# A transformer block on one core: last chunk of batch 1 finished inside the MLP, first search in other banks, second search's last turn one block later

## The chip, the cores and the metric

The kernel runs on one core of a Trainium2 chip. The metric is device time in microseconds (us); before the change it is 2070.14 us, the median of 3 runs (2069.56 to 2070.2). Engines are named as in the profile: PE multiplies matrices, DVE and ACT work on tiles, POOL does small vector work and issues indirect DMAs, SP issues plain DMAs.

## The reference

Two batches of 4096 tokens, 256 features, float32. A tokenizer with a 4096 x 4096 gate, then attention over heads with gates, then a feed-forward layer through which only the best half of the tokens goes:

```python
h = tok(x)                                    # (2, 4096, 256)
h = h + attn(layernorm(h))                    # 8 heads, sigmoid gate, residual
z = layernorm(h)
weights = z @ wr + br                         # one router weight for each token
_, idx = top_k(weights, 2048); sel_idx = idx[:, :2047]
y = (gelu(z[sel_idx] @ w1 + b1) @ w2 + b2) * w_sel      # hidden width 1024
out = h + z;  out[sel_idx] += y
```

## The kernel before

The tokenizer and the weights of the heads fill the first 1670 us or so and are not touched here. Two stages follow.

**mix** runs over 8 chunks of 512 tokens, both batches `s` = 0 and 1 in each (a tile row `[h, s]`, `h` being the parity of the chunk). PE makes values, gates and the output projection (`project`, into banks 0 to 3, `products`). For a chunk and batch DVE then runs `moments` (residual added to `rows`, mean and variance) and `route` (router weight, stored in `rows` and kept in `router`, counted by `mx_w_kept`); POOL runs `scale` between the two (reciprocal root of the variance, shift); ACT runs `norm` (the normalized row plus residual, `base`); SP stores `rows` to `scratch["rows"]` and `base` to the output. A chunk's batch 1 is finished two steps after it was begun, so (chunk 7, batch 1) comes last of all.

**mlp** takes the best tokens. `TopRows` finds them on DVE and PE for a batch `b`: ten turns; DVE counts (L1258, L1261), PE adds the counts over partitions (`pe_turn`, L1348), DVE goes on (`dve_advance`). Turns 0 to 7 find the threshold digit by digit, turn 8 the ranks, and turn 9 takes a large comparison on DVE (`dve_lanes`, L1317) and 32 small products on PE (L1354), from which `dve_list` makes the list of rows (`top_rows`). It uses `CB`, bank 2, and `TIES`, bank 3.

The first search (b = 0) runs alone (`dve_all(0)`), then POOL gathers the first three units of 512 rows (`gather(0)` to `gather(2)`, four indirect DMAs each), ACT normalizes unit 0 (`norm`), PE turns it (`turn`), ACT and DVE split it in high and low parts (`split`), and the MLP begins: 8 units `u` of 8 blocks `j`, in all 64 blocks, `g = 8u + j`. In this text H(g) is the first layer's product of block g (6 matmuls, L1588) and S(g) the second layer's (12 matmuls, L1568); PE's order is H(g), a turn of the second search if there is one, S(g - 2), and at j = 4 the turning of the next unit. Between H and S, ACT makes Gelu and its high part, DVE the low part `act_lo` (L1534). POOL's `base(u)` (L1428) adds the normalized rows to the gathered ones; `base(0)` stands behind `gather(2)` in POOL's order.

The second search (b = 1) is spread over these blocks: a stage on DVE at every second g (`search`), PE's turn n in block g = 2n + 2. Turn 9 is thus in block 20, its comparison on DVE in block 19, and the list in block 20. `gather(4)`, the first of batch 1, waits for that list.

Waits are on semaphores, in each engine's program order; the order is written by hand.

Of the kernel before, what the change touches and what calls it, by code (L numbers as in the profile page):

```python
# [5 lines left out]
P = 128  # L6
# [879 lines left out]
def mix(pr, W2, M, products, room, scratch, router, mlp_raw, W3):  # L886
# [3 lines left out]
    with ExitStack() as ctx:  # L890
        m_hi, m_lo, V, GB = (M[n] for n in ("m_hi", "m_lo", "V", "GB"))
        h_in, rows = (room[n] for n in ("h_in", "rows"))
        base, late = sb(nc, ctx, "base", [P, 2, 2, TPC, D]), sb(nc, ctx, "late", [P, 8 * CH])
# [15 lines left out]
        block = pr.block  # L909

# [50 lines left out]
        def _(act):  # L961
# [28 lines left out]
            def step(c, h):  # L990
# [3 lines left out]
                if within(c, 2):  # L994
                    norm(c - 2, h, 1)
# [15 lines left out]
            chunks(step)  # L1011

        @block.vector
        def _(dve):
# [45 lines left out]
            def step(c, h):  # L1060
                if within(c, 2):
                    moments(c - 2, h, 1)
# [4 lines left out]
                if within(c, 2):  # L1067
                    route(c - 2, h, 1)
# [12 lines left out]
            chunks(step)  # L1081

        @block.gpsimd
        def _(pool):
# [52 lines left out]
            def step(c, h):  # L1137
                if within(c, 2):
                    scale(c - 2, h, 1)
# [14 lines left out]
            chunks(step)  # L1154

        @block.tensor
        def _(pe):
# [29 lines left out]
            chunks(step)  # L1187

# [6 lines left out]
class TopRows:  # L1195
# [8 lines left out]
    def __init__(self, pr, W2, W3, router, sbuf, K):  # L1204
# [20 lines left out]
        self.CB, self.TIES = pr.banks[2], pr.banks[3]  # L1225
# [37 lines left out]
    def dve_advance(self, b, q):  # L1263
# [4 lines left out]
        link(v.scalar_tensor_tensor(self.reach[:, :], self.CB[:, 0:PIV], float(self.K), self.W3["step"][:, q % STEPS, :],  # L1268
# [90 lines left out]
def mlp(pr, W2, W3, ident, scratch, router):  # L1359
# [9 lines left out]
    with ExitStack() as ctx:  # L1369
# [16 lines left out]
        all_rows = scratch["rows"].rearrange("b c j p e -> (b c j p) e")  # L1386
        out_rows = pr.out.rearrange("b t d -> (b t) d")
# [22 lines left out]
        def _(pool):  # L1410
            def gather(u):
# [4 lines left out]
                for j in range(TPC):  # L1416
                    nc.gpsimd.indirect_dma_start(taken[:, u % HELD, j, :], None, all_rows, offsets(u, j)).then_inc(
# [13 lines left out]
            for u in range(HELD):  # L1431
# [12 lines left out]
        def _(act):  # L1444
# [14 lines left out]
            for b in range(B):  # L1459
                stored(act, b)  # L1460
            for j in range(TPC):
                norm(0, j)
            split(0)
            for u in range(U):
                for j in range(FT):
# [5 lines left out]
                    act.wait_ge(gelu_ok, u * FT + j + 1)  # L1471
# [7 lines left out]
        def _(dve):  # L1479
# [33 lines left out]
            def search(g):  # L1513
# [37 lines left out]
        def _(pe):  # L1551
# [164 lines left out]
```

## Time and profile before

| | |
|---|---|
| median of 3 runs | 2070.14 us |
| the profiled execution | 2072.95 us, its span 2071.2 us |
| busy, share of the span | PE 96%, DVE 59%, ACT 33%, POOL 22% |
| chain that ended last, by engine | PE 90%, DVE 4%, issue 2%, ACT 2%, POOL 1% |
| granted clock, mean over the span | 0.977 of full speed |

The span runs from the first to the last instruction; 1.75 us of the profiled execution lie around it. The granted clock is that of PE, as a share of 2.4 GHz: 0.50 is its lower level of 1.2 GHz. Times of rows are microseconds from the span's start.

### The profile page before, as it was taken

The numbers are of one execution on the slowest core, as the hardware profiler recorded it, in microseconds if no ns is written. First come the engines' busy times: TensorE is split into PE (matmuls) and PEld (weight loads), VectorE is DVE, ScalarE is ACT, GpSimd is POOL, SyncE is SP. The second block draws the span as 40 slices with busy tenths as digits, with TensorE's granted clock in tenths as the row PEclk, the third lists the DMA queues.
The fourth block names the chain that finished last, engine by engine and source line by source line (L and its number), as shares of the span: only waits on it lengthen the run. The fifth ranks groups of instructions, "written<-read, shape, count | busy, mean of one in ns | idle before, by whom it ended". The sixth has DMA issues, their size and how long they took to land.

```text
span 2071.2 us, 27479 instructions
## 1 busy us (share of the span) xinstructions
PE 1988.7 (96%) x9534; PEld 1646.7 (80%) x9534; DVE 1222.2 (59%) x2220; ACT 675.0 (33%) x1093; POOL 451.0 (22%) x578
## 2 busy tenths in 40 slices
PE   7999999999999999999999999999999989829998
PEld 6888888888888888888888888888887878718897
DVE  4656565665656556656565665656554358756553
ACT  4422222222222225422222222222222147524454
POOL 3302020202202023312020201202023057532342
PEclk9999999999999999999999999999999989959999
DMA  4232433334243333242433334243334469620110
GB/s 143 88 105 73 162 112 122 112 122 145 75 164 112 122 112 132 72 153 81 154 112 123 111 122 150 73 162 112 112 112 143 148 241 313 220 77 22 42 42 31
DMA packets 88114, 250.14 MB, mean 121 GB/s; under 512 B 11968, under 2 KB 32448, under 8 KB 88000
## 3 DMA queue, kind: packets, MB, share of 16 engines
q1 hardware_dynamic: 84928, 240.27, 34.5%
q0 software_dynamic: 3072, 8.44, 1.3%
q8 instruction: 61, 1.00, 0.2%
q14 instruction: 53, 0.43, 0.1%
HBM read 194.05 MB, written 54.62 MB: 120 GB/s over the span
## 4 chain that ended last, share of the span: by engine, by line
PE 90%; DVE 4%; issue 2%; ACT 2%; POOL 1%; DMA 0%; SPq 0%; DVEq 0%; ACTq 0%; POOLq 0%
PE bank L663 34%; PE bank L678 34%; PE bank L1568 4%; PE bank L810 4%; PE bank L1588 4%; PE bank L713 3%; PE bank L1169 2%; PE bank L635 1%; PE bank L609 1%; PE bank L619 1%; DVE kt L482 0%; DVE vf L493 0%; PE bank L648 0%; ACT work L380 0%; PE bank L836 0%
## 5 line engine op out<-in xcount | busy, mean ns | idle before, releaser
L678 PE MATMUL bank<-x_hi,kt 128*128 128x512 f32 x2048 | 724.0, 395 | 1.5 <-DVE work L519 1.4
L519 DVE SCALAR_TENSOR_TENSOR work<-bank,d_col,gate 128x512 f32<-128x512 f32 x512 | 383.8, 750 | 553.7 <-PE bank L678 544.7
L398 ACT ACTIVATE p_hi<-work 128x512 fp32r<-128x512 f32 x512 | 324.1, 633 | 1065.5 <-PE bank L663 1024.9
L678 PEld LDWEIGHTS bank<-x_hi,kt 128*128 128x128 f32 x2048 | 384.4, 188 | 90.4 <-DVE work L519 2.4
L663 PE MATMUL bank<-p_hi,v_hi 128*128 128x512 f32 x1024 | 407.0, 397 | 0.3 <-ACT yT L360 0.2
L663 PE MATMUL bank<-p_hi,v_lo 128*128 128x512 f32 x1024 | 404.2, 395 | 0.0
L663 PE MATMUL bank<-p_lo,v_hi 128*128 128x512 f32 x1024 | 403.4, 394 | 0.0
L678 PE MATMUL bank<-x_lo,kt 128*128 128x512 f32 x1024 | 401.0, 392 | 0.0
L507 DVE TENSOR_TENSOR p_lo<-work,p_hi 128x512 fp32r<-128x512 f32 x512 | 367.4, 718 | 29.3 <-ACT p_hi L398 29.2
L568 POOL TENSOR_SCALAR spread<-mv 128x4 f32<-128x4 f32 x16 | 4.9, 308 | 1125.4 <-DVE mv L451 1125.4
L663 PEld LDWEIGHTS bank<-p_hi,v_hi 128*128 128x128 f32 x1024 | 192.2, 188 | 50.6 <-DVE p_lo L507 5.3
L663 PEld LDWEIGHTS bank<-p_hi,v_lo 128*128 128x128 f32 x1024 | 192.3, 188 | 46.3
L663 PEld LDWEIGHTS bank<-p_lo,v_hi 128*128 128x128 f32 x1024 | 193.2, 189 | 44.7
L678 PEld LDWEIGHTS bank<-x_lo,kt 128*128 128x128 f32 x1024 | 192.3, 188 | 43.4
L1534 DVE TENSOR_TENSOR act_lo<-act,act_hi 128x512 fp32r<-128x512 f32 x64 | 59.2, 925 | 91.0 <-ACT act_hi L1472 90.8
L1568 PE MATMUL bank<-ffn,act_hi 128*128 128x256 f32 x512 | 97.4, 289 | 0.0
L1588 PE MATMUL bank<-fx_hi,ffn 128*128 128x512 f32 x256 | 92.5, 408 | 2.2 <-DVE fx_lo L1483 2.2
L1568 PEld LDWEIGHTS bank<-ffn,act_hi 128*128 128x128 f32 x512 | 84.2, 194 | 4.3 <-DVE act_lo L1534 0.2
L575 POOL TENSOR_TENSOR mn_sb<-mn_sb,gamma 128x256 f32<-128x256 f32 x64 | 55.2, 893 | 98.7 <-DVE mn_sb L456 98.7
L1568 PE MATMUL bank<-ffn,act_lo 128*128 128x256 f32 x256 | 73.6, 288 | 0.0
L713 PE MATMUL bank<-kt 128*128 128x256 f32 (+1 forms) x384 | 68.3, 339 | 2.2 <-DVE kt L544 2.2
L713 PEld LDWEIGHTS bank<-kt 128*128 128x128 f32 x384 | 59.2, 189 | 11.2 <-DVE kt L544 2.9
(226 smaller groups left out, 2271.7 us busy)
## 6 DMA issues: line engine op xcount, KB each, us to landing
gate<-in_gateT SPq DMA_DIRECT2D x256, 512.0 KB, 3.6
work<-in_xT SPq DMA_DIRECT2D x32, 512.0 KB, 4.7
scratch_rows<-rows SPq DMA_DIRECT2D x16, 518.0 KB, 4.0
scratch_h<-work SPq DMA_DIRECT2D x16, 512.0 KB, 3.0
scratch_mn<-mn_sb SPq DMA_DIRECT2D x16, 512.0 KB, 6.8
scratch_mT_hi<-mT_hi SPq DMA_DIRECT2D x16, 512.0 KB, 2.7
scratch_mT_lo<-mT_lo SPq DMA_DIRECT2D x16, 512.0 KB, 4.0
gate<-scratch_mn SPq DMA_DIRECT2D x16, 512.0 KB, 4.2
```

The source lines that it names most:

```text
L398: nc.scalar.activation(p_hi[:, i % 2, :], p32[:, i % RP, :], ACT.Copy).then_inc(hi_done, 1)
L507: nc.vector.tensor_tensor(p_lo[:, i % 2, :], p32[:, i % RP, :], p_hi[:, i % 2, :].bitcast(F32), ALU.subtract).then_inc(lo_done, 1)
L519: nc.vector.scalar_tensor_tensor(p32[:, i % RP, :], S[i % 2][:, :], d_col[:, i:i + 1], gate[:, g % RG, j, :], ALU.add, ALU.mult).then_inc( ...
L575: nc.gpsimd.tensor_tensor(mn_sb[:, j, :], mn_sb[:, j, :], W["gamma"][:, :], ALU.mult).then_inc(scaled, 1)
L663: mm = pe.matmul(Y[m][:, :], v, p, start=i == 0 and n == 0, stop=i == ST - 1 and n == 2)
L678: mm = pe.matmul(S[i % 2][:, :], w, x, start=n == 1, stop=n == 3 * KD)
L713: mm = pe.matmul(out, w, x, start=early(c, 1) and j == 0 and n == 0, stop=False, skip_group_check=True)
L810: mm = pe.matmul(bank[:, :], ww, x, start=i == 1, stop=i == 3 * pr.KD)
L1169: mm = pe.matmul(products[:, j, 0:D + 2], x, w, start=i == 0, stop=i == 3 * KD - 1)
L1534: nc.vector.tensor_tensor(a_lo[:, j % 2, :], act32[:, j % 2, :], a_hi[:, j % 2, :].bitcast(F32), ALU.subtract).then_inc(al_ok, 1)
L1568: mm = pe.matmul(YB[t // 2][:, (t % 2) * D:(t % 2 + 1) * D], a, w, start=j == 0 and t % 2 == 0 and n == 0, stop=j == FT - 1 and n == 2, sk ...
L1588: mm = pe.matmul(HB[j % 2][:, :], w, x, start=n == 1, stop=n == 3 * KD)
```

## The change

What `moments`, `scale`, `route` and `norm` do for (chunk 7, batch 1) is taken out of mix and put into mlp as functions that mix returns. The first search starts without them. It uses banks 4 and 5, since banks 0 to 3 still hold the projection of that chunk. A Gelu on one column is issued on ACT ahead of the first unit. The second search's turn 9 and its list are put one block and two blocks later. Some tiles are allocated further out, so that they live into mlp; the order in which the head weights' tiles are allocated changes with it. `gather` reads from a view that ends with the rows of its batch.

```diff
@@ mix: ACT, DVE and POOL, in step()
-                if within(c, 2):
+                if within(c, 2) and c - 2 < NC - 1:
                     norm(c - 2, h, 1)
...
+            last["norm"] = lambda: norm(NC - 1, (NC - 1) % 2, 1)
...
+            last["moments"] = lambda: moments(NC - 1, (NC - 1) % 2, 1)
+            last["route"] = lambda: route(NC - 1, (NC - 1) % 2, 1)
...
+            last["scale"] = lambda: scale(NC - 1, (NC - 1) % 2, 1)
@@ TopRows
-        self.CB, self.TIES = pr.banks[2], pr.banks[3]
+        self.CB, self.TIES = (pr.banks[4], pr.banks[2]), (pr.banks[5], pr.banks[3])
@@ mlp, POOL
-            for u in range(HELD):
+            gather(0)
+            last_chunk["scale"]()
+            for u in range(1, HELD):
                 gather(u)
             base(0)
@@ mlp, ACT
-            for b in range(B):
-                stored(act, b)
+            stored(act, 0)
+            nc.scalar.activation(act32[:, 0, 0:1], W3["b1"][:, 0:1], ACT.Gelu_apprx_tanh).then_inc(gelu_ok, 1)
             for j in range(TPC):
                 norm(0, j)
             split(0)
+            last_chunk["norm"]()
@@ mlp, DVE
-                elif g == 4 * STEPS + 4:
+                elif g == 4 * STEPS + 6:
                     top.dve_list(1)
...
+            dve.wait_ge(pr.sem("mx_w_kept"), B * pr.NC - 1)
+            top.dve_all(0)
+            last_chunk["moments"]()
+            stored(dve, 0)
+            split(0)
+            last_chunk["route"]()
             dve.wait_ge(pr.sem("mx_w_kept"), B * pr.NC)
-            top.dve_all(0)
-            for b in range(B):
-                stored(dve, b)
-            split(0)
@@ mlp, PE
-            pe.wait_ge(pr.sem("mx_h2_ok"), 4 * pr.NC)
             for i in range(top.TURNS):
                 top.pe_turn(0, i)
             turn(0)
+            pe.wait_ge(pr.sem("mx_h2_ok"), 4 * pr.NC)
+            pe.wait_ge(pr.sem("mx_raw_ok"), 2 * pr.NC)
...
-                    if j % 2 == 0 and 0 <= n < top.TURNS:
+                    if j % 2 == 0 and 0 <= n < top.TURNS - 1:
                         top.pe_turn(1, n)
+                    if u * FT + j == 2 * top.TURNS + 1:
+                        top.pe_turn(1, top.TURNS - 1)
```

On DVE, around the end of the first search: before, the last chunk's rows (`rows<-bank,h_in` to `router`) stand ahead of the search's first row (`top_zero`); this is where mix ends and mlp begins.

```order
L1057 TENSOR_TENSOR router<-w_mid,rows 128x4
L1035 TENSOR_TENSOR rows<-bank,h_in 128x2x256 [waits mx_op,mx_st_x11,mx_h_ld1]
L1035 TENSOR_TENSOR rows<-bank,h_in 128x2x256 [waits mx_op]
L1037 TENSOR_TENSOR w_raw<-bank,h_router 128x4
L1042 BN_STATS stats<-rows 128x6 [waits mx_h2_ok] x4
L1046 BN_AGGR mv<-stats 128x2 [waits mx_st_ok] x4
L1052 SCALAR_TENSOR_TENSOR w_mid<-mv,sum_wr,w_raw 128x4 [waits mx_raw_ok,mx_mv_ok]
L1056 TENSOR_TENSOR rows<-w_mid,rows 128x4 [waits mx_mid_ok,mx_rs_ok]
L1057 TENSOR_TENSOR router<-w_mid,rows 128x4
L1478 UNCONDITIONAL_BRANCH
L1239 MEMSET top_zero 128x32 [waits mx_w_kept,mw_made]
```

With the change the same rows on DVE stand behind the list of the first search (`top_rows`), and `split` of unit 0 (`fx_lo`) parts them.

```order
L1331 SCALAR_TENSOR_TENSOR top_rows<-bank,top_low_part 128x16 [waits top_chain]
L1037 TENSOR_TENSOR rows<-bank,h_in 128x2x256 [waits mx_op,mx_st_x11,mx_h_ld1]
L1037 TENSOR_TENSOR rows<-bank,h_in 128x2x256 [waits mx_op]
L1039 TENSOR_TENSOR w_raw<-bank,h_router 128x4
L1044 BN_STATS stats<-rows 128x6 [waits mx_h2_ok] x4
L1048 BN_AGGR mv<-stats 128x2 [waits mx_st_ok] x4
L1494 TENSOR_TENSOR fx_lo<-bank,fx_hi 128x512 [waits ff_hi_ok,mx_st_x01,mx_st_x00]
L1494 TENSOR_TENSOR fx_lo<-bank,fx_hi 128x512 [waits ff_hi_ok]
L1054 SCALAR_TENSOR_TENSOR w_mid<-mv,sum_wr,w_raw 128x4 [waits mx_raw_ok,mx_mv_ok]
L1058 TENSOR_TENSOR rows<-w_mid,rows 128x4 [waits mx_mid_ok,mx_rs_ok]
L1059 TENSOR_TENSOR router<-w_mid,rows 128x4
L1547 TENSOR_TENSOR act_lo<-act,act_hi 128x512 [waits ff_ah_ok,mx_w_kept]
```

Eight rows of DVE have moved past the search, three of them past the split too; the next `act_lo` waits for them.

On POOL, with the change, the five rows of `scale` stand between the first four indirect DMAs and the other eight (before, all twelve stood in a row, behind `scale`).

```order
L1425 DMA taken<-scratch_rows,top_rows 128x259 [waits top_rows_ok,mx_st_x01,mx_st_x00]
L1425 DMA taken<-scratch_rows,top_rows 128x259 x3
L1130 TENSOR_SCALAR spread<-mv 128x4 [waits mx_mv_ok]
L1133 TENSOR_TENSOR rows<-spread,power 128x4 [waits mx_sp_ok,mx_power_ok]
L1135 TENSOR_TENSOR rows<-mv,rows 128x4 [waits mx_rs_ok]
L1136 TENSOR_SCALAR rstd_plus<-rows 128x4
L1139 TENSOR_SCALAR rows<-rows 128x4 [waits mx_r1_ok]
L1425 DMA taken<-scratch_rows,top_rows 128x259 x8
L1436 TENSOR_TENSOR taken<-taken,xn 128x4x256 [waits ff_xn_ok] x2
```

The eight later DMAs and the first `base` (the last row) come behind the five rows now.

On PE before, in blocks 20 and 21 of the MLP: the small products of turn 9 stand right behind H(20), ahead of S(18), of the turning of unit 3 and of H(21).

```order
L1588 MATMUL bank<-fx_hi,ffn 128x512
L1354 MATMUL bank<-top_numbers,top_in_lane 128x32 [waits top_counted]
L1354 MATMUL bank<-top_numbers,top_in_lane 128x32 x31
L1568 MATMUL bank<-ffn,act_hi 128x256 [waits ff_al_ok]
L1568 MATMUL bank<-ffn,act_hi 128x256
```

With the change they stand behind H(21), ahead of S(19).

```order
L1602 MATMUL bank<-fx_hi,ffn 128x512 [waits ff_gelu_ok]
L1602 MATMUL bank<-fx_lo,ffn 128x512
L1602 MATMUL bank<-fx_hi,ffn 128x512 x2
L1602 MATMUL bank<-fx_lo,ffn 128x512
L1602 MATMUL bank<-fx_hi,ffn 128x512
L1361 MATMUL bank<-top_numbers,top_in_lane 128x32 [waits top_counted]
L1361 MATMUL bank<-top_numbers,top_in_lane 128x32 x31
L1581 MATMUL bank<-ffn,act_hi 128x256 [waits ff_al_ok]
```

S(18), the turning of unit 3 and H(21) have moved ahead of the wait for `top_counted`.

## Rows read from the trace of the kernel before

**Rows 1.** Timeline of DVE: start, us, what, [idle before <-releaser]; first search's ends.

```profile
1810.88 0.18 DVE L1057 TENSOR_TENSOR router<-w_mid,rows 128x4 f32<-128x4 f32 x1
...
1815.69 0.18 DVE L1057 TENSOR_TENSOR router<-w_mid,rows 128x4 f32<-128x4 f32 x1
1816.02 0.09 DVE L1239 MEMSET top_zero<- 128x32 f32 x1
...
1844.49 0.17 DVE L1324 SCALAR_TENSOR_TENSOR top_rows<-bank,top_low_part 128x16 int32<-128x16 f32 x1
```

**Rows 2.** Timeline of POOL: scale of (chunk 7, batch 1), indirect DMAs, base(0), gather(4).

```profile
1814.16 0.23 POOL L1126 TENSOR_SCALAR spread<-mv 128x4 f32<-128x4 f32 x1 [2.60 <-DVE mv L1046]
...
1816.14 0.23 POOL L1135 TENSOR_SCALAR rows<-rows 128x4 f32<-128x4 f32 x1
1845.61 1.25 POOL L1417 DMA_INDIRECT taken<-scratch_rows,top_rows  x1 [29.24 <-DVE top_rows L1324]
...
1859.69 0.95 POOL L1417 DMA_INDIRECT taken<-scratch_rows,top_rows  x1 [0.30 <-issue]
1860.66 2.21 POOL L1428 TENSOR_TENSOR taken<-taken,xn 128x1024 f32<-128x1024 f32 x1
...
1935.72 0.97 POOL L1417 DMA_INDIRECT taken<-scratch_rows,top_rows  x1 [10.95 <-DVE top_rows L1324]
```

**Rows 3.** Timeline of ACT: norm of (chunk 7, batch 1), first normalized rows, table, Gelu.

```profile
1816.47 2.07 ACT L967 ACTIVATE base<-rows,rstd_plus 128x256 f32<-128x256 f32 x4 [2.74 <-POOL rows L1135]
1848.79 0.60 ACT L1456 ACTIVATE xn<-taken 128x256 f32<-128x256 f32 x1 [30.25 <-DMA taken<-scratch_rows,top_rows]
...
1854.93 1.28 ACT L1468 ACT_TABLE_LOAD   x1
1858.92 0.69 ACT L1468 ACTIVATE act<-bank,b 128x512 f32<-128x512 f32 x1 [2.71 <-PE bank L1588]
```

**Rows 4.** Timeline of PE: H(0), first turn of the second search, H(4).

```profile
1855.99 0.76 PE L1588 MATMUL bank<-fx_hi,ffn 128*128 128x512 f32 x1 [2.20 <-DVE fx_lo L1483]
...
1865.65 0.20 PE L1348 MATMUL bank<-top_counts,ones 128*128 128x15 bf16 x1 [2.77 <-DVE top_counts L1261]
...
1872.69 0.39 PE L1588 MATMUL bank<-fx_hi,ffn 128*128 128x512 f32 x1
```

**Rows 5.** Windows: length, PE, PEld, DVE, ACT, POOL busy, granted clock, DMA, GB/s.

```profile
1865.60:1871.50 5.90, 5.85 (x22) 5.28 (x23) 3.34 (x13) 1.42 (x3) 0.00 (x0) 0.50 0.01 3
...
1926.00:1933.00 7.00, 5.02 (x45) 5.02 (x46) 1.92 (x1) 0.00 (x0) 0.00 (x0) 0.52 0.00 0
```

**Rows 6.** Timeline of DVE: act_lo of blocks 0 and 1, the second search's first counts.

```profile
1860.30 3.13 DVE L1534 TENSOR_TENSOR act_lo<-act,act_hi 128x512 fp32r<-128x512 f32 x1 [4.46 <-ACT act_hi L1472]
...
1864.49 0.41 DVE L1258 TENSOR_TENSOR top_passed<-top_left,grid 128x480 bf16<-128x480 uint16 x1
1864.93 0.66 DVE L1261 TENSOR_REDUCE top_counts<-top_passed 128x15 bf16<-128x480 bf16 x1
...
1866.39 0.69 DVE L1534 TENSOR_TENSOR act_lo<-act,act_hi 128x512 fp32r<-128x512 f32 x1
```

**Rows 7.** Timeline of PE: end of H(20), turn 9, S(18), S(19).

```profile
1923.79 0.40 PE L1588 MATMUL bank<-fx_hi,ffn 128*128 128x512 f32 x1
1927.98 2.34 PE L1354 MATMUL bank<-top_numbers,top_in_lane 128*128 128x32 bf16 x32 [3.80 <-DVE top_in_lane L1317]
1930.13 0.78 PE L1568 MATMUL bank<-ffn,act_hi 128*128 128x256 f32 x2
...
1935.23 0.40 PE L1568 MATMUL bank<-ffn,act_hi 128*128 128x256 f32 x2
```

**Rows 8.** Chain that ended last, in order of time: an S and an H.

```profile
1878.09 1.42 PE bank L1568 x12
1879.51 1.40 PE bank L1588 x6
```

**Rows 9.** Timeline of DVE, block 19: the large comparison.

```profile
1925.64 2.28 DVE L1317 TENSOR_TENSOR top_in_lane<-top_lane_b,lanes 128x4096 bf16<-128x4096 bf16 x1
```

More of the change, by code:

```diff
@@ L883, in _, with mix @@
         nc.scalar.activation(expd[:, :, :, :], shifted[:, :, :, :], ACT.Exp, scale=scale).then_inc(exp_ok, 1)
-def mix(pr, W2, M, products, room, scratch, router, mlp_raw, W3):
+def mix(pr, W2, M, products, room, scratch, router, mlp_raw, W3, L):
     nc, ins, D, KD, NC = pr.nc, pr.ins, pr.D, pr.KD, pr.NC
@@ L892, in mix @@
         h_in, rows = (room[n] for n in ("h_in", "rows"))
-        base, late = sb(nc, ctx, "base", [P, 2, 2, TPC, D]), sb(nc, ctx, "late", [P, 8 * CH])
+        late = sb(nc, ctx, "late", [P, 8 * CH])
+        base, stats, mv, spread, rstd1, w_raw, w_mid, power = (L[n] for n in (
+            "base", "stats", "mv", "spread", "rstd_plus1", "w_raw", "w_mid", "power"))
         og_hi, og_lo = (sb(nc, ctx, n, [P, 2, 2, KD, CH], F32R) for n in ("og_hi", "og_lo"))
@@ L909, in mix @@
         block = pr.block
+        last = {}
         def rstd(h, s):
@@ L1060, in step @@
             def step(c, h):
-                if within(c, 2):
+                if within(c, 2) and c - 2 < NC - 1:
                     moments(c - 2, h, 1)
@@ L1066, in step @@
                     mixed(c, 0)
-                if within(c, 2):
+                if within(c, 2) and c - 2 < NC - 1:
                     route(c - 2, h, 1)
@@ L1137, in step @@
             def step(c, h):
-                if within(c, 2):
+                if within(c, 2) and c - 2 < NC - 1:
                     scale(c - 2, h, 1)
@@ L1187, in _ @@
             chunks(step)
+        return last
 STEPS = 4
@@ L1347, in pe_turn, with mlp @@
         if i < 2 * STEPS:
-            mm = pe.matmul(self.CB[:, 0:PIV], ones, self.counts[:, :], start=True, stop=True)
+            mm = pe.matmul(self.CB[b][:, 0:PIV], ones, self.counts[:, :], start=True, stop=True)
         elif i == 2 * STEPS:
-            pe.matmul(self.TIES[:, 0:2 * ST + 2], before, self.of_b[:, :], start=True, stop=False)
-            mm = pe.matmul(self.TIES[:, 0:2 * ST + 2], ones, self.earlier_b[:, :], start=False, stop=True)
+            pe.matmul(self.TIES[b][:, 0:2 * ST + 2], before, self.of_b[:, :], start=True, stop=False)
+            mm = pe.matmul(self.TIES[b][:, 0:2 * ST + 2], ones, self.earlier_b[:, :], start=False, stop=True)
         else:
             for t in range(ST):
-                mm = pe.matmul(self.CB[:, 0:2 * self.Q], self.in_lane[:, :, t], self.numbers[:, :, t], start=t == 0,
+                mm = pe.matmul(self.CB[b][:, 0:2 * self.Q], self.in_lane[:, :, t], self.numbers[:, :, t], start=t == 0,
                                stop=t == ST - 1)
         mm.then_inc(self.summed, 1)
-def mlp(pr, W2, W3, ident, scratch, router):
+def mlp(pr, W2, W3, ident, scratch, router, last_chunk):
     nc, ins, D, KD, ST, F, B = pr.nc, pr.ins, pr.D, pr.KD, pr.ST, pr.F, pr.B
@@ L1386, in mlp @@
         all_rows = scratch["rows"].rearrange("b c j p e -> (b c j p) e")
+        up_to = [all_rows[0:(b + 1) * pr.T] for b in range(B)]
         out_rows = pr.out.rearrange("b t d -> (b t) d")
@@ L1580, in _ @@
                 for j in range(FT):
[L1581 removed]
+                    past(pe, gelu_ok, u * FT + j if u * FT + j > 1 else 0)
                     cols = slice(j * P, (j + 1) * P)
@@ L1652, in build @@
         room = {n: sb(nc, ctx, n, [P, 2, 2, TPC, width + e]) for n, e in (("h_in", 0), ("rows", EXTRA))}
+        L = {"base": sb(nc, ctx, "base", [P, 2, 2, TPC, width]), "stats": sb(nc, ctx, "stats2", [P, 2, 2, TPC, 6]),
+             "mv": sb(nc, ctx, "mv2", [P, 2, 2, TPC, 2]), "power": sb(nc, ctx, "power2", [P, TPC])}
+        for n in ("spread", "rstd_plus1", "w_raw", "w_mid"):
+            L[n] = sb(nc, ctx, f"{n}2", [P, 2, 2, TPC])
         ffn = sb(nc, ctx, "ffn", [P, 4 * KD * hidden], F32R)
@@ L1675, in build @@
             products = psum[:, 0:TPC * CH].rearrange("p (j n) -> p j n", j=TPC)
-            mix(pr, W2, M, products, room, scratch, router, mlp_raw, W3)
-        mlp(pr, W2, W3, ident, scratch, router)
+            last_chunk = mix(pr, W2, M, products, room, scratch, router, mlp_raw, W3, L)
+        mlp(pr, W2, W3, ident, scratch, router, last_chunk)
 def _layouts(inputs):
```

20 lines of the change are left out of this document (8 added, 12 removed).

## The prediction, before the changed kernel was run

> **What bounds the kernel now.** I read the mean clock and the chain first (PE 90% of it), then the timelines of the engines from the end of mix to block 21. Up to 1810 the change touches nothing, and once the MLP runs PE is the bound: a block is one S and one H. So what counts is where PE stands still after 1810, and there are three such places.
>
> First, the first search. It begins on DVE at 1816.02, right behind the last chunk's router row, and its list is done at 1844.66 [rows 1]; POOL's first indirect DMA follows 0.95 us later, and ACT has the first rows 3.2 us after that issue began [rows 2, 3]. PE gets H(0) at 1855.99 [rows 4]. The chain is DVE's alone, then POOL's and the DMA's.
>
> Second, the first turn of the second search: PE waits 2.77 us for DVE's counts in block 2 [rows 4], and the stretch behind it, 1865.6 to 1871.5, runs at clock 0.50, the lower level of 1.2 GHz, although PE is busy in it [rows 5]. DVE is late because `act_lo` of block 0 took 3.13 us where the next one took 0.69 [rows 6]: POOL's `base(0)`, 1860.66 to 1862.87 [rows 2], lies over it.
>
> Third, turn 9: PE waits 3.80 us for the large comparison [rows 7], and again the clock is 0.52 afterwards, 1926 to 1933 [rows 5].
>
> **The change part by part.** I write t0 for the start of H(0): 1855.99 before, to be found for after.
>
> *A, the first search starts earlier.* Before, DVE ends the router row of (chunk 7, batch 0) at 1811.06 and that of (chunk 7, batch 1) at 1815.87, and starts the search 0.15 later [rows 1]. With the second of these gone from the front, the search starts at 1811.21: 4.8 us earlier, and its list with it, at 1839.85. Nothing in the search waits for the moved work: its products use banks 4 and 5. The eight moved rows of DVE now run from 1839.85 for 3 us (1810.99 to 1814.0 before), while DVE would only wait for the rows to land; the split of unit 0 is due some 10 us after the list. Their cost is nothing. PE's H(0) additionally waits for the residual's two semaphores, which are up by 1843. The one cost I can't exclude: the first four indirect DMAs are issued while DVE is busy. Issues take between 0.95 and 1.25 us in these rows, so it is 0 to 0.5 in all; I take 0, as DVE's moved rows are mostly done when the third issue begins. A is 4.3 to 4.8, and t0 becomes 1851.2.
>
> *The rest of the last chunk.* POOL's `scale` takes 2.2 us (1814.16 to 1816.37), between the fourth issue and the fifth [rows 2]. Twelve issues are 1.28 us apart, so the fourth ends at 1845.8 after the shift, `scale` at 1848.0, and the other eight issues begin 0 to 0.9 us later (the bound is the 0.95 ahead of the first). Unit 1's first rows then land near t0 + 0.5; ACT wants them only after its first Gelu, t0 + 4.2. ACT's `norm` takes 2.07 us and stands where the table load of 1.28 us stood, between the split and the first Gelu; there ACT idles 2.71 us after the load [rows 3], so 0.8 us more is covered. For the same reason loading Gelu's table early is worth 0: the load was hidden behind H(0). DVE's `route` (0.5 us) lies under H(0), and the `act_lo` behind it is not due before t0 + 4.3. SP stores the chunk near t0 + 1; behind it SP has only the loads of b2, wanted eight blocks on, over 20 us later.
>
> *B, the first turn of the second search.* `scale` also pushes `base(0)` back: eight issues end 10 us after the fifth begins, so `base(0)` starts at 1858.1 to 1858.9, t0 + 6.9 to 7.7, where it was t0 + 4.7. `act_lo` of block 0 starts at t0 + 4.31 as before and now takes 0.69. From its end to the end of the counts DVE needs 2.16 us (1863.43 to 1865.59 [rows 6]): t0 + 7.16. PE ends H(2) at t0 + 6.89 (1865.65 less the wait), so the wait is 0.3 us in place of 2.77, and I expect no fall of the clock: the trace has shorter waits in later blocks without one. At full clock S(0), H(3) and S(1) take 1.42 + 1.40 + 1.42 [rows 8]; from t0 + 7.26 that puts H(4) at t0 + 11.5, against t0 + 16.70 before [rows 4]: 5.2 us. What is late next is `act_lo` of block 1, behind the rest of the key's preparation on DVE, on which `base(0)` now falls: it holds one of those rows until t0 + 9.1 to 10.0, then come 0.7 us of small rows and 0.69, so t0 + 10.5 to 11.4 against S(1)'s wish of t0 + 10.1. I take 0.6 off (0 to 1.3): B is 4.6, between 3.9 and 5.2.
>
> The Trainium skill, on its page "SBUF — State Buffer", section "Who interferes with whom", says that a DVE instruction with two SBUF inputs fully blocks against a GpSimd one that reads SBUF, and that a reduce never contends on trn2. The trace agrees on the first, with 3.13 against 0.69; no row here shows a reduce under POOL's work. By that rule a `base(0)` that starts inside the counts' reduce (t0 + 6.5 to 7.2) costs them nothing and B stays 4.6; were a reduce held too, B would be near 0 for such a start and the sum 9.9.
>
> *C, turn 9 one block later.* H(20)'s last matmul starts at 1923.79, the next could at 1924.03. With turn 9 out of the way PE goes on with S(18), 1.42, whose `act_lo` is long done, the turning of unit 3, 0.9, and H(21), 1.40: 1927.75. The comparison ends at 1927.92 [rows 9], so turn 9 starts at 1927.98 as before, after a wait of 0.2 in place of 3.80. The 32 small products take 2.15 us to the next start (1930.13 [rows 7]), so S(19) starts at 1930.13 in place of 1935.23: C is 5.1. They were measured at the lower clock; if they halve with it as the big ones do, C is 6.1. I take 5.1, the measured row. The list now comes behind `act_lo` of block 22, some 1.4 us later in these times, so `gather(4)` starts near 1937.1 for 1935.72 [rows 2]; its first rows land 3.2 us later, 1940.3, and ACT wants them after the high part of block 24, near 1940.8. It fits, with 0.5 us, and ACT has 1.6 us more before a Gelu is late.
>
> Sum: 4.8 + 4.6 + 5.1 = 14.5 us. The profiled execution took 2072.95 us, 1.75 of it outside the span; it becomes 2058.4. The median of the runs lies 2.8 us below the profiled one, so I predict 2055.6. The bounds give 4.8 + 5.2 + 6.1 = 16.1 and 4.3 + 3.9 + 4.7 = 12.9 (0.4 off C for a list or a comparison that is later): 2054.0 to 2057.2.
>
> **The rivals.**
>
> *`base(0)` meets the counts.* For: by my own times it misses the end of L1258 (t0 + 6.5) by only 0.4 us, and `act_lo` was held although its row starts 0.36 ahead of `base(0)`'s. Against: the issues' spacing is regular. If POOL is faster by half a microsecond, the counts wait for `base(0)`, PE waits its 2.7 us as before and the clock falls as before: B is 0, gain 9.9, 2060.2. Chance 0.18.
>
> *The clock falls at one of the two places all the same.* For: after turn 9's 2.15 us of 32-column products, with 0.2 us of waiting, PE has done little for 2.4 us, and the two waits that were followed by 0.50 were 2.77 and 3.80. Against: it is not idle in them. A stretch like that of 1865.6 to 1871.5 costs half of 5.9, 2.9 us: 2058.5. Chance 0.18.
>
> *Batch 1's gather is late.* If the list and four DMAs come more than 2.1 us later than I have them, PE waits in unit 3 or 4 for each microsecond beyond; 2 to 4 us, 2058 to 2060. Chance 0.04.
>
> *Slower: POOL doesn't go straight from `scale` back to indirect DMAs.* `gather(1)` then lands late, and ACT, which has unit 1's rows ahead of its second Gelu, stands, and PE with it. The cover is 3.7 us (t0 + 0.5 to t0 + 4.2). Each microsecond beyond is lost; past 18 us of delay the gain is gone, past 22 the kernel is slower by more than 0.2%. Against: POOL goes from the twelfth issue to `base(0)` within 0.02 us (1860.64 to 1860.66), and the way back from another wait takes 0.95 [rows 2]. Chance 0.02.
>
> *The search is not what PE waits for at the start.* Then A is nothing. But the first issue follows the list by 0.95 us and waits for nothing later, and its row names the list alone as what ended POOL's wait [rows 2]. Chance 0.02, gain 9.7, 2060.4.
>
> **How the numbers follow.** My forecast has 0.56, its own range is 2054.0 to 2057.2. The first two rivals take 0.36 and lie at 2060.2 and 2058.5, so the range reaches from 2053.6 (the bound and the spread of the runs) to 2061.0; both together (2063.1), and slower, are left out. About 0.2%, 4.1 us, is what a measurement of this kernel can tell from no change. All rivals but the fourth and a mixture of several gain more than that: faster 0.93, within 0.2% 0.05, slower 0.02.
>
> **What would show it.** A: the search's first row near 1811.2 and H(0) near 1851.2. B: `act_lo` of block 0 at 0.69 us, a first turn with a wait below 1 us, no 0.50 after H(2), H(4) within 12.5 us of t0; `base(0)` near t0 + 7.3. C: turn 9 with a wait below 0.5 and a clock of 1.00 behind it. The load of Gelu's table should appear during the search and save nothing. I am wrong if `gather(1)` or `gather(4)` becomes the releaser of ACT, or if POOL's order makes H(0) later than 1852.

## The result and the profile after

The changed kernel takes 2056.99 us, the median of 6 runs (2055.52 to 2060.18); the kernel before, on the same chip, 2070.17 us (6 runs, 2069.29 to 2074.19). The ratio is 0.9935, 95% interval 0.9924 to 0.9945: some 13 us less. The forecast was 2055.6 us. The profiled execution of the changed kernel took 2060.18 us, with a span of 2058.5 and a clock of 0.981; its span is 12.7 us below that of before. As before, I write t0 for the start of H(0).

DVE's timeline (start, us, what), from the end of mix to turn 9's comparison, answers to [rows 1, 6, 9]:

```profile
1810.53 0.18 DVE L1059 TENSOR_TENSOR router<-w_mid,rows 128x4 f32<-128x4 f32 x1
1810.85 0.09 DVE L1246 MEMSET top_zero<- 128x32 f32 x1
...
1839.34 0.17 DVE L1331 SCALAR_TENSOR_TENSOR top_rows<-bank,top_low_part 128x16 int32<-128x16 f32 x1
1839.45 1.29 DVE L1037 TENSOR_TENSOR rows<-bank,h_in 128x512 f32<-128x512 f32 x2
...
1842.04 0.41 DVE L1048 BATCH_NORM_AGGREGATE mv<-stats 128x2 f32<-128x6 f32 x4
...
1855.28 0.69 DVE L1547 TENSOR_TENSOR act_lo<-act,act_hi 128x512 fp32r<-128x512 f32 x1 [4.06 <-ACT act_hi L1483]
...
1857.57 0.66 DVE L1268 TENSOR_REDUCE top_counts<-top_passed 128x15 bf16<-128x480 bf16 x1
1858.14 2.18 DVE L1256 CAST top_key<-top_part 128x32 f32<-128x32 int32 x1
...
1916.30 2.29 DVE L1324 TENSOR_TENSOR top_in_lane<-top_lane_b,lanes 128x4096 bf16<-128x4096 bf16 x1
```

The search starts right behind the router row that used to be the last but one: 1810.85 for 1816.02. `act_lo` of block 0 has gone from 3.13 to 0.69. The long row is now the CAST of `top_key`, 2.18 (0.17 for the same row in the first search, at 1813.30), which no engine waits for directly. POOL's timeline shows why, and answers to [rows 2]:

```profile
1844.53 0.95 POOL L1425 DMA_INDIRECT taken<-scratch_rows,top_rows  x1 [0.30 <-issue]
1845.55 0.23 POOL L1130 TENSOR_SCALAR spread<-mv 128x4 f32<-128x4 f32 x1
...
1847.55 0.23 POOL L1139 TENSOR_SCALAR rows<-rows 128x4 f32<-128x4 f32 x1
1848.12 1.11 POOL L1425 DMA_INDIRECT taken<-scratch_rows,top_rows  x1 [0.34 <-issue]
...
1858.05 2.21 POOL L1436 TENSOR_TENSOR taken<-taken,xn 128x1024 f32<-128x1024 f32 x1
...
1929.60 0.97 POOL L1425 DMA_INDIRECT taken<-scratch_rows,top_rows  x1 [14.16 <-DVE top_rows L1331]
```

`scale` runs between the issues, POOL goes back to them after 0.34 us, and `base(0)` starts at t0 + 7.16, inside the counts' reduce. PE's timeline answers to [rows 4, 7]:

```profile
1850.89 0.77 PE L1602 MATMUL bank<-fx_hi,ffn 128*128 128x512 f32 x1 [2.21 <-DVE fx_lo L1494]
...
1858.28 0.18 PE L1355 MATMUL bank<-top_counts,ones 128*128 128x15 bf16 x1 [0.60 <-DVE top_counts L1268]
...
1861.78 0.51 PE L1581 MATMUL bank<-ffn,act_hi 128*128 128x256 f32 x2 [0.41 <-DVE act_lo L1547]
...
1863.31 0.39 PE L1602 MATMUL bank<-fx_hi,ffn 128*128 128x512 f32 x1
...
1918.17 0.40 PE L1602 MATMUL bank<-fx_hi,ffn 128*128 128x512 f32 x1
1918.65 2.44 PE L1361 MATMUL bank<-top_numbers,top_in_lane 128*128 128x32 bf16 x32
1920.90 0.72 PE L1581 MATMUL bank<-ffn,act_hi 128*128 128x256 f32 x2
```

The wait of 2.77 is now 0.60, and one of 0.41 for `act_lo` of block 1 has come behind it. The 3.80 is gone: turn 9 starts 0.06 after the comparison ends (1916.30 + 2.29 = 1918.59). But the last row shows something else: 0.72 for two products that take 0.40 at full clock [rows 7]. Windows of the same kernel (length; busy us of PE, PEld, DVE, ACT, POOL; clock; DMA share; GB/s) for block 2, the small products, and S(19) with H(22):

```profile
1857.00:1862.00 5.00, 3.98 (x23) 2.92 (x23) 4.69 (x10) 3.03 (x7) 3.16 (x2) 1.00 0.60 113
...
1918.65:1920.90 2.25, 2.25 (x33) 2.25 (x33) 0.54 (x1) 0.65 (x1) 0.00 (x0) 1.00 0.03 7
1920.90:1925.33 4.43, 4.43 (x21) 4.07 (x20) 0.88 (x2) 1.54 (x3) 0.00 (x0) 0.61 0.00 0
```

No 0.50 in block 2 any more [rows 5]. Behind turn 9 the clock still falls, though PE has not waited: 4.43 us for work that takes 1.42 + 1.40 = 2.82 [rows 8], so 1.6 us.

ACT's timeline answers to [rows 3]; Gelu's table is loaded during the search, and the norm of the last chunk stands where the load stood before:

```profile
1816.39 1.28 ACT L1470 ACT_TABLE_LOAD   x1 [3.02 <-DMA out<-base]
...
1849.69 2.06 ACT L968 ACTIVATE base<-rows,rstd_plus 128x256 f32<-128x256 f32 x4
...
1853.83 0.69 ACT L1479 ACTIVATE act<-bank,b 128x512 f32<-128x512 f32 x1 [2.07 <-PE bank L1602]
```

### The profile page after: what moved, and what is told of

It reads as the page before. It is cut to its first block, busy times and chain, and to the rows that moved or that the text cites. A ratio compares the mean times of both kernels' runs of the same rounds, so it can differ in the third digit from the quotient of the medians.

```text
span 2058.5 us, 27479 instructions
## 1 busy us (share of the span) xinstructions
PE 1986.8 (97%) x9534; PEld 1644.2 (80%) x9534; DVE 1219.7 (59%) x2220; ACT 675.1 (33%) x1094; POOL 453.7 (22%) x578
## 4 chain that ended last, share of the span: by engine, by line
PE 90%; DVE 4%; issue 2%; ACT 2%; POOL 1%; DMA 0%; SPq 0%; DVEq 0%; ACTq 0%; POOLq 0%
PE bank L663 35%; PE bank L678 34%; PE bank L1581 4%; PE bank L810 4%; PE bank L1602 4%; PE bank L713 3%; PE bank L1174 2%; PE bank L635 1%; PE bank L609 1%; PE bank L619 1%; DVE kt L482 0%; DVE vf L493 0%; PE bank L648 0%; ACT work L380 0%; PE bank L836 0%
## 5 line engine op out<-in xcount | busy, mean ns | idle before, releaser
L1547 DVE TENSOR_TENSOR act_lo<-act,act_hi 128x512 fp32r<-128x512 f32 x64 | 54.5, 853 | 85.5 <-ACT act_hi L1483 85.3
```

What stands on the lines that cost most here:

```text
L1547: nc.vector.tensor_tensor(a_lo[:, j % 2, :], act32[:, j % 2, :], a_hi[:, j % 2, :].bitcast(F32), ALU.subtract).then_inc(al_ok, 1)
```

## Experiments

The theory is the prediction's: A, B and C are three separate gains, B since `base(0)` no longer meets `act_lo`, C since turn 9 no longer waits. The times of one kernel spread over 3 to 7 us, more than some of the terms. The reading that tells them apart is in the profiles: how far each place of PE's order is from the one before. Every row of this table is from one profiled execution: the start of the first search (`top_zero`), of H(0) and of H(4), and the end of the span.

| kernel | search starts | H(0), t0 | H(4) - t0 | end - H(4) |
|---|---|---|---|---|
| before | 1816.02 | 1855.99 | 16.70 | 198.5 |
| changed | 1810.85 | 1850.89 | 12.42 | 195.2 |
| changed, again (e9) | 1808.77 | 1848.75 | 12.66 | 195.1 |
| e1, before + later turn 9 | 1814.24 | 1854.20 | 15.59 | 193.6 |
| e2, changed with turn 9 back | 1808.85 | 1848.77 | 12.69 | 198.7 |
| e3, before + other place of `base(0)` | 1816.09 | 1856.05 | 11.60 | 198.8 |
| e4, changed, `base(0)` meets `act_lo` | 1808.89 | 1848.90 | 14.00 | 193.5 |
| e5, changed, small products spread | 1811.54 | 1851.46 | 12.69 | 194.5 |
| e6, changed, `base(0)` early | 1811.21 | 1850.98 | 11.67 | 193.7 |
| e7, changed without the early table | 1809.22 | 1849.23 | 12.64 | 193.5 |
| e8, e5 + e6 + early first stage | 1811.26 | 1851.16 | 10.13 | 194.4 |
| e8, again (e10) | 1810.88 | 1850.86 | 10.15 | 194.5 |
| e11, e8 without spreading | 1810.16 | 1850.13 | 11.08 | 193.6 |

From the search's start to t0 it is 39.8 to 40.0 us in all of them. The start itself varies by 1.9 us among kernels with the old order and by 2.8 among those with the new one; a good part of the spread of the times arises there. The last router row ahead of the search (1810.53 in the changed kernel) is that of (chunk 7, batch 0). It starts at 1808.44 to 1811.21 in the ten profiles with the new order, and at 1809.10 to 1810.95 in the three with the old, so no gain ahead of it, for instance from the changed order of the head weights' tiles, is seen. From that row to t0 it is 45.10 or 45.11 us with the old order and 40.1 to 40.4 with the new. That is A, read in thirteen profiles; no run has A alone or leaves only A out.

One more thing moves H(4) - t0, and it is not part of the change. The clock is 0.50 behind t0 in every profile, and comes up to 1.00 between t0 + 3 and t0 + 4 in e1, e3, e5, e6, e8 and e10, but between t0 + 5 and t0 + 6 in the other seven. Where PE waits in block 2, the wait takes this up; where it waits for nothing there, H(4) shifts by about 0.9 us (e10 against e11 below).

**e1: turn 9 and its list one and two blocks later, all else as before.**

```diff
-                elif g == 4 * STEPS + 4:
+                elif g == 4 * STEPS + 6:
                     top.dve_list(1)
...
-                    if j % 2 == 0 and 0 <= n < top.TURNS:
+                    if j % 2 == 0 and 0 <= n < top.TURNS - 1:
                         top.pe_turn(1, n)
+                    if u * FT + j == 2 * top.TURNS + 1:
+                        top.pe_turn(1, top.TURNS - 1)
```

> The kernel before, with turn 9 one block and its list two blocks later, nothing else. Theory (three separate gains): H(0) and the 2.77 us wait in block 2 stay; PE's wait for the large comparison falls from 3.80 us to about 0.2; from H(4) to S(19) 57.6 us in place of 62.5, then a stretch at clock 0.50 that gives back 1.6: gain 3.3 to 5.0 us, near 2066. Rival (the gain at turn 9 needs the earlier start, for instance because the clock's state at that place differs): the wait goes but less than 2 us are gained, near 2069.

Measured: 2065.13 us, ratio 0.9975 (0.9966 to 0.9984), 5.2 us less. Its PE timeline:

```profile
1863.88 0.18 PE L1348 MATMUL bank<-top_counts,ones 128*128 128x15 bf16 x1 [3.50 <-DVE top_counts L1261]
...
1925.05 2.44 PE L1354 MATMUL bank<-top_numbers,top_in_lane 128*128 128x32 bf16 x32
...
1927.32 0.49 PE L1568 MATMUL bank<-ffn,act_hi 128*128 128x256 f32 x2
```

```profile
1864.00:1870.00 6.00, 6.00 (x32) 5.43 (x32) 3.25 (x12) 1.82 (x4) 0.00 (x0) 0.72 0.01 3
```

The wait in block 2 and the fall behind it stay (the window has clock 0.72). The wait is longer than before because PE came to it sooner, with the clock up between t0 + 3 and t0 + 4; the counts come at the same place, t0 + 9.68 for 9.66. Turn 9's wait is gone, and here the clock stays up behind turn 9 (0.49 in place of 0.72). C alone is 198.5 - 193.6 = 4.9 us.

**e2: the changed kernel with turn 9 back in block 20.**

```diff
-                elif g == 4 * STEPS + 6:
+                elif g == 4 * STEPS + 4:
                     top.dve_list(1)
...
-                    if j % 2 == 0 and 0 <= n < top.TURNS - 1:
+                    if j % 2 == 0 and 0 <= n < top.TURNS:
                         top.pe_turn(1, n)
-                    if u * FT + j == 2 * top.TURNS + 1:
-                        top.pe_turn(1, top.TURNS - 1)
```

> The changed kernel with turn 9 and its list put back into block 20. Theory: H(0) near 1851 and the short wait of 0.6 us in block 2 stay; the wait of 3.8 us before turn 9 and the stretch at 0.5 behind it come back; 3.3 to 5.0 us slower than the changed kernel, near 2061. Rival (the gains overlap): as fast as the changed kernel within 1 us.

Measured: 2062.28 us, 0.9962 (0.9949 to 0.9976), which is 5.6 us behind the changed kernel's ratio. PE's timeline and a window behind turn 9:

```profile
1916.70 2.38 PE L1361 MATMUL bank<-top_numbers,top_in_lane 128*128 128x32 bf16 x32 [3.80 <-DVE top_in_lane L1324]
```
```profile
1918.90:1925.00 6.10, 6.10 (x35) 5.83 (x34) 0.95 (x3) 1.14 (x2) 0.51 (x1) 0.71 0.01 3
```

The same 3.80 and the fall behind it are back: C from the other side, 198.7 - 195.2 = 3.5 us against this kernel's own fall, 5.1 against the 193.6 of a turn 9 without one.

**e3: before, with `base(0)` between `gather(1)` and `gather(2)`.**

```diff
-            for u in range(HELD):
-                gather(u)
+            gather(0)
+            gather(1)
             base(0)
+            gather(2)
```

> The kernel before, with base(0) on POOL put between the second and the third unit's indirect DMAs, so that it is over before act_lo of block 0; the last chunk and turn 9 stay where they were. Theory (base(0) held act_lo, and that made the wait and the fall of the clock): act_lo of block 0 takes 0.69 us, PE's wait in block 2 is 0.5 in place of 2.77, no stretch at 0.50 behind it, H(4) at 11.5 to 12 us after H(0) in place of 16.7, and the whole gain of 4.5 to 5 us with it: near 2065.5. Rival (the wait has another cause, for instance the router rows or the first search's end): act_lo or the wait stays above 2 us and the time is that of before.

Measured: 2066.93 us, 0.9979 (0.997 to 0.9988), 4.4 us less. POOL, DVE and PE in its timelines:

```profile
1855.75 2.18 POOL L1428 TENSOR_TENSOR taken<-taken,xn 128x1024 f32<-128x1024 f32 x1
```
```profile
1860.36 0.69 DVE L1535 TENSOR_TENSOR act_lo<-act,act_hi 128x512 fp32r<-128x512 f32 x1 [4.46 <-ACT act_hi L1473]
...
1863.14 0.22 DVE L1249 CAST top_key<-top_part 128x32 f32<-128x32 int32 x1
```
```profile
1863.29 0.18 PE L1348 MATMUL bank<-top_counts,ones 128*128 128x15 bf16 x1 [1.01 <-DVE top_counts L1261]
```
```profile
1863.29:1868.00 4.71, 4.71 (x33) 4.41 (x34) 3.39 (x13) 2.00 (x5) 0.07 (x1) 1.00 0.11 32
```

With `base(0)` done before `act_lo` starts, `act_lo` takes 0.69, the CAST 0.22, and the fall is gone (clock 1.00 from 1863.29 to 1868). So another place of `base(0)`, without anything else of the change, is enough for B: 16.70 - 11.60 = 5.1 us here.

**e4: the changed kernel with `base(0)` two DMAs earlier**, so that it meets `act_lo` again.

```diff
                 for j in range(TPC):
+                    if u == 2 and j == 2:
+                        base(0)
                     nc.gpsimd.indirect_dma_start(taken[:, u % HELD, j, :], None, up_to[u // NU], offsets(u, j)).then_inc(
...
             for u in range(1, HELD):
                 gather(u)
-            base(0)
```

> The changed kernel with base(0) put behind the second of the third unit's four indirect DMAs, so that it starts near 1855.5, when act_lo of block 0 starts too (1855.3). Theory: act_lo is held to 3 us, PE waits 2.5 to 2.8 us for the counts, the clock falls to 0.50 behind it, H(4) comes 16 to 17 us after H(0) in place of 12.4; about 4 us slower than the changed kernel, near 2061. Rival (whoever starts first has the port, and act_lo starts 0.2 us ahead): act_lo takes 0.69 and the time is that of the changed kernel.

Measured: 2059.88 us, 0.9951 (0.9936 to 0.9966); the interval overlaps the changed kernel's. DVE, POOL, PE, and a window behind the wait:

```profile
1853.29 3.02 DVE L1548 TENSOR_TENSOR act_lo<-act,act_hi 128x512 fp32r<-128x512 f32 x1 [4.06 <-ACT act_hi L1484]
```
```profile
1853.54 2.21 POOL L1438 TENSOR_TENSOR taken<-taken,xn 128x1024 f32<-128x1024 f32 x1
```
```profile
1858.54 0.18 PE L1355 MATMUL bank<-top_counts,ones 128*128 128x15 bf16 x1 [2.83 <-DVE top_counts L1268]
```
```profile
1858.50:1864.00 5.50, 5.46 (x36) 5.04 (x37) 3.60 (x14) 2.72 (x5) 0.11 (x1) 1.00 0.14 42
```

The 3 us row and the wait are back with the meeting, although `act_lo`'s row starts 0.25 us ahead of `base(0)`'s. The clock did not fall behind this wait of 2.83, though it fell behind 2.77 [rows 4, 5] and behind e1's 3.50. H(4) is 1.3 to 1.6 us later than in the changed kernel, where the forecast had it about 4 us later: the wait alone is worth that much. The other 2.7 to 2.9 of the 4.3 between the kernel before and the changed one go with the fall of the clock, as half of the 5.9 us at 0.50 [rows 5] would have it. So the meeting explains the wait; why the clock fell behind it in the kernel before and not here is open.

**e5: the changed kernel, turn 9's 32 products four at a time behind the quarters of S(19) and S(20).**

```diff
-            def second(u, j):
+            def second(u, j, part=-1):
...
+                    if 0 <= part < 2:
+                        top.pe_lanes(1, (part * TPC + t) * ST // (2 * TPC), (part * TPC + t + 1) * ST // (2 * TPC))
...
-                        top.pe_turn(1, top.TURNS - 1)
+                        pe.wait_ge(top.counted, 2 * top.TURNS)
...
-                        second(u, j - LAG)
+                        second(u, j - LAG, u * FT + j - 2 * top.TURNS - 1)
```

`pe_lanes` issues the products of `pe_turn`'s turn 9 from the first given column of lanes to the second.

> The changed kernel with turn 9's 32 small products spread, four behind each quarter of S(19) and of S(20), in place of all 32 ahead of S(19). Theory (the stretch at half clock after turn 9 comes from 2.2 us in which PE does only small products, and is seen in some executions and not in others): no half clock behind S(19) in the profile, H(23) not later than in the changed kernel, 0 to 1.6 us faster, near 2056. Rival (mixed with the large products the small ones cost more than in a row, for each break in the stream): S(19) and S(20) together take more than 2.84 + 2.2 us, and the time is 1 us or more above the changed kernel.

Measured: 2059.55 us, 0.9939 (0.9925 to 0.9954): no gain to be seen. The clock stays at 1.00 from 1915 to 1930, but end - H(4) is 194.5: 0.7 better than the changed kernel with its fall, 0.9 worse than a turn 9 in a row without one. Spread products cost something themselves. In the PE timeline of e10, which spreads them in the same way, a quarter of S(19) with its four takes 0.74 us (1917.10 to 1917.84), where one without takes 0.36 (1920.90 to 1921.26 in e4), so the 32 cost about 8 x 0.38 = 3.0 us in place of 2.25:

```profile
1917.10 0.48 PE L1590 MATMUL bank<-ffn,act_hi 128*128 128x256 f32 x2
1917.42 0.28 PE L1590 MATMUL bank<-ffn,act_lo 128*128 128x256 f32 x1
1917.54 0.48 PE L1368 MATMUL bank<-top_numbers,top_in_lane 128*128 128x32 bf16 x4
1917.84 0.48 PE L1590 MATMUL bank<-ffn,act_hi 128*128 128x256 f32 x2
```

**e6: the changed kernel, `base(0)` right behind `scale`, ahead of `gather(1)`.**

```diff
             last_chunk["scale"]()
+            base(0)
             for u in range(1, HELD):
                 gather(u)
-            base(0)
```

> The changed kernel with base(0) right behind the last chunk's scale, ahead of the second unit's indirect DMAs. Theory: base(0) runs near 2.8 us before H(0) ends its wait, where DVE has only the split with one operand in PSUM; the copy of the key behind the counts takes 0.2 us in place of 2.18, S(1) has no wait of 0.4 us, H(4) comes 11.6 to 12.0 us after H(0) in place of 12.4; 0.4 to 0.8 us faster, which the times alone may not show. Rival (the second unit's DMAs, 2.3 us later, make ACT and so PE wait): ACT waits for taken rows in block 0 or 1 and H(4) comes later than 12.4.

Measured: 2058.0 us, 0.9936 (0.9923 to 0.995). POOL and PE:

```profile
1848.11 2.17 POOL L1436 TENSOR_TENSOR taken<-taken,xn 128x1024 f32<-128x1024 f32 x1
```
```profile
1858.29 0.18 PE L1355 MATMUL bank<-top_counts,ones 128*128 128x15 bf16 x1 [1.25 <-DVE top_counts L1268]
```

`base(0)` starts at 1848.11 and nothing on DVE is held (the CAST takes 0.22, the split's two rows 1.29 as before); H(4) comes at t0 + 11.67, 0.75 to 1 us earlier than in the changed kernel. What remains is a wait of 1.25 us for DVE's own rows ahead of the counts.

**e7: the changed kernel without the one-column Gelu.**

```diff
-            nc.scalar.activation(act32[:, 0, 0:1], W3["b1"][:, 0:1], ACT.Gelu_apprx_tanh).then_inc(gelu_ok, 1)
...
-                    act.wait_ge(gelu_ok, u * FT + j + 2)
+                    act.wait_ge(gelu_ok, u * FT + j + 1)
...
-                    past(pe, gelu_ok, u * FT + j if u * FT + j > 1 else 0)
+                    past(pe, gelu_ok, u * FT + j - 1)
```

The two waits on `gelu_ok` count one Gelu less.

> The changed kernel without the Gelu on one column, so that the table is loaded ahead of the first real Gelu again. Theory (the load is hidden there too): ACT does norm of the last chunk and the load between the split and H(0)'s end, 2.06 + 1.28 us in a gap of 4.1, first Gelu right at H(0)'s end as before, time that of the changed kernel within 0.5 us. Rival (the early load is part of the gain): first Gelu late by up to 1.3 us, H(4) later than 12.4 us after H(0).

Measured: 2057.53 us, 0.9938 (0.9924 to 0.9952). ACT's timeline:

```profile
1850.11 1.28 ACT L1478 ACT_TABLE_LOAD   x1
1852.17 0.69 ACT L1478 ACTIVATE act<-bank,b 128x512 f32<-128x512 f32 x1 [0.77 <-PE bank L1601]
```

Behind the late load ACT still waits 0.77 us for PE, so the load is hidden either way, and the early one is worth 0.

**e8: e5, e6 and the second search's first stage on DVE ahead of `act_lo` of block 0.** Beside those two edits:

```diff
-                if g % 2 == 0 and n <= 2 * STEPS:
+                if g % 2 == 0 and 0 < n <= 2 * STEPS:
...
             dve.wait_ge(pr.sem("mx_w_kept"), B * pr.NC)
+            top.dve_stage(1, 0)
```

> The two edits before (turn 9 spread, base(0) early) and one more: the second search's first stage (its keys and first counts) on DVE ahead of act_lo of block 0, where DVE waits 4 us for ACT. Theory: the first turn finds its counts ready, PE has no wait in block 2 and none before S(1), H(4) 11.0 to 11.4 us after H(0); with 0 to 1.6 us at turn 9 in all 1 to 3 us faster than the changed kernel, near 2055. Rival (PE is bound by ACT there, which must finish the high part of block 0 after S(0)): H(4) not before 11.8 and no gain beyond that of base(0).

Measured: 2057.93 us, 0.9932 (0.9919 to 0.9946). PE waits neither for the first turn nor ahead of S(1), and H(4) is 2.3 us earlier than in the changed kernel, at t0 + 10.13 for a forecast of 11.0 to 11.4. About 0.9 of this is the clock, which came up 2 us sooner after t0 than in the changed kernel (e11, with the clock late, has 11.08). The median does not show the rest.

**e9, e10, e11** ran on one chip: the changed kernel again, e8 again, and e8 without the spreading of e5 (so e6's edit and the early first stage).

> The changed kernel once more, unchanged. Question: is the fall of the clock behind the moved turn 9 a property of the kernel or of one execution? Measure: MLP length, from the start of H(0) to the span's end (207.6 us in the first profile of the changed kernel, of which 1.6 behind turn 9). If it belongs to the execution (my theory, as four of five profiles with the same turn 9 showed none): full clock behind turn 9 and some 206.0 us. If it belongs to the kernel: clock 0.81 again and 207.6. The time by itself says little, as the first search starts up to 2.5 us earlier or later in profiles of one kernel.

> The version with all three improvements (small products spread, base(0) ahead of gather(1), the second search's first stage ahead of act_lo of block 0) once more, now on the same chip as the changed kernel. By the MLP length of its first profile, 204.5 us, against 206.0 to 207.6 for the changed kernel, it should be 1.5 to 3 us faster: ratio to the changed kernel 0.9985 to 0.9993. The rival, that what is saved in block 2 is lost later or is less than the spread of runs, expects medians within 1 us.

> The same without spreading the small products. If the spread products cost something of their own (they lie between big products of S(19) and S(20)) this one is as fast as or faster than e10: MLP length 204.5 or less, if the clock stays up behind turn 9; H(4) at t0 + 10.1 as there. If spreading is what keeps the clock up, some of its executions should fall to 0.5 behind turn 9 and take 1.6 us more.

Measured: 2060.08 us, 0.9941 (0.9927 to 0.9954); 2057.24 us, 0.9933 (0.9919 to 0.9946); 2057.37 us, 0.9935 (0.9921 to 0.9948). In e9 the clock fell behind turn 9 again. Windows over its small products, and over S(19) and H(22):

```profile
1916.72:1918.99 2.27, 2.27 (x32) 2.27 (x33) 0.54 (x1) 0.63 (x1) 0.00 (x0) 1.00 0.00 0
1918.99:1923.40 4.41, 4.41 (x21) 4.11 (x20) 0.80 (x2) 1.46 (x3) 0.00 (x0) 0.61 0.02 4
```

I had expected the fall not to come back; that was wrong. In both profiles of the changed kernel it is there, in e1, e4, e6, e7 and e11, with the same turn 9 in a row, it is not. So it does not belong to the turn as such, and two profiles against five are too few to tell a property of the changed kernel from chance; e7 differs from the changed kernel only in when Gelu's table is loaded, 1850.11 for 1816.39, long before turn 9. From t0 to the end e10 and e11 take 204.6 and 204.7 us, the changed kernel 207.6 and 207.8: 3 us less in the profiles. But about 1.5 of these are the fall: e7, with none, takes 206.2. Their medians are 2.8 and 2.7 us below e9's, but the intervals overlap, and the changed kernel's first six runs had 2056.99. So the profiles speak for a version better by 1.5 us, or by 3 where the changed kernel's clock falls, and the times don't show one. e11's H(4) is 0.9 later than e10's since the clock came up to full later after H(0). Windows from t0 + 3 to t0 + 4, of e10 and of e11:

```profile
1853.86:1854.86 1.00, 1.00 (x5) 0.78 (x5) 0.39 (x4) 0.97 (x2) 0.69 (x2) 0.83 1.10 373
```
```profile
1853.13:1854.13 1.00, 1.00 (x4) 0.71 (x4) 0.39 (x4) 0.97 (x2) 0.69 (x2) 0.50 1.11 363
```

e11 makes this up by its 32 products in a row.

## Why the prediction held, point by point

**A, 4.8.** Right. The search starts 0.32 us behind the router row of 1810.53, where before it was 5.14 behind that of 1810.88 [rows 1]: 4.8 less, and so it is in every profile of either order. And t0 was forecast for 1851.2 and came at 1850.89. The moved rows cost nothing, as counted: DVE is done with the moments at 1842.45 and idle until the split.

**The rest of the last chunk, 0.** Right: `scale` was forecast from 1845.8 to 1848.0 and ran from 1845.55 to 1847.78; the norm lies in ACT's gap; the table load is worth 0 by e7. `gather(4)` came in time: no row of ACT waits for it. The rivals of a late gather and a slow return of POOL did not come up (0.34 us).

**B, 4.6.** The mechanism is shown by e3, and by e4 for the wait, though not for the fall of the clock; the size is 4.0 to 4.3: the first turn waits 0.60, not 0.3, and S(1) then 0.41 (in e9 0.45 and 0.74), inside the bounds of 3.9 to 5.2. `base(0)` starts at t0 + 7.16, and 0.5 us after the end of L1265, so the rival that it meets the counts missed by as little as the prediction said; no run has `base(0)` start inside L1265, so what that would cost is not shown. The reduce took 0.66, as without `base(0)` [rows 6], but only its last 0.18 us lie under it; the CAST behind it took 2.18 for 0.22 in e3. The Trainium skill, on "SBUF — State Buffer", section "Who interferes with whom", says that a reduce never contends with GpSimd on trn2, while a cast can, in a mode in which it takes the ports that the two engines share; the CAST agrees, and the reduce does not speak against it, though 0.18 us of overlap hardly test it.

**C, 5.1.** The wait went as worked out, and so did the products: H(4) to S(19) is 62.54 us before (1872.69 to 1935.23) and 57.59 after (1863.31 to 1920.90), 4.95 less. The bound of 6.1 is refuted: the 32 products take 2.25 us at clock 1.00 and 2.15 to 2.20 at 0.50 (the first in the kernel before, below, the second in e2), so they do not follow the clock.

```profile
1927.98:1930.13 2.15, 2.15 (x32) 2.15 (x33) 0.00 (x0) 0.00 (x0) 0.00 (x0) 0.50 0.00 0
```

**The step that failed** is the one behind turn 9: a clock of 1.00, with "it is not idle in them" against the fall. The fall came in both profiles of the changed kernel: it is the second rival, at 1.6 us, about half of its price of 2.9. With it the profiled sum is 5.1 (t0; 0.35 of it arose ahead of the change) + 4.28 + 4.95 - 1.63 = 12.7, as in the spans, against 14.5 forecast and a lower bound of 12.9. The medians are 13.2 us apart, inside the bounds, and the new one lies 1.4 us above its forecast. That fits the fall, but the profiled execution is the slowest of the six, and for the other five no row shows whether their clock fell. So the mechanism of A, B and C held; that the median stayed in the forecast's own range, with 0.2 us to spare, owes something to luck. Why the clock falls there in this kernel and not in e7 stays open.

## What to carry to other kernels

A short wait of the bounding engine can cost twice: the wait, and the stretch at the lower clock behind it; take both from the rows, and give the second a chance of its own also where a run of tiny products takes the wait's place. A large addition on POOL stretched rows of DVE that read only SBUF, `act_lo` to 3.0 to 3.1 us and the CAST to 2.2 to 2.5, and not the split, which reads a bank too (1.29 for two rows in e6, with 0.74 us under `base(0)`). What this costs depends on who waits: in the changed kernel `act_lo` is held to 3.04 to 3.13 us in four later blocks (first at 1895.92), and PE waits for none of them. So place such an instruction under a row of DVE that nobody waits for. When the terms are smaller than the spread of the times, measure between two fixed places of the order in the profiles, as t0, H(4) and the end here: these distances repeat within 0.3 us, as long as the clock is the same in them, while the times spread by 3 to 7.

## What was not expected of the hardware

- Behind a wait of 2.83 us the clock stayed at 1.00 (e4), behind one of 2.77 it fell to 0.50 [rows 4, 5]; behind 2.25 us of 32-column products without any wait it fell in 2 profiles of 7. The length of the wait alone does not decide. Nor did the fall come at one place: before, the clock was down while PE still waited (0.50 from 1864.99 to 1865.65); in e1 PE had worked again for about 1 us (clock 1.00 from 1863.88, where the wait ended, to 1864.88, and 0.50 in the microsecond behind).
- DVE's `act_lo` was stretched to 3.02 us although its row starts 0.25 us ahead of POOL's `base(0)` (e4), like 3.13 with 0.36 before; the CAST takes 2.50 in e9, with its row 0.24 us ahead. The Trainium skill, on the same page and section, says that the order of issue decides who blocks; by the starts of these rows it would have been POOL, so here the starts of rows do not tell that order, or the rule does not hold for this pair.
- The 32 products of 32 columns take 2.15 us at clock 0.50 and 2.25 at 1.00: no gain from the clock.
